# Probabilities of the second attention layer: turned by DMA instead of TensorE, scores first, weighted sums after

## The chip, the cores and the metric

The kernel runs on one core of a Trainium2 chip. The time is the device time of one execution in microseconds (us); three runs of the kernel before are shown by their median. TensorE (PE) multiplies matrices, VectorE (DVE) and ScalarE (ACT) do elementwise work and reductions, GpSimd (POOL) does elementwise work in SBUF, and SyncE (SP) issues the DMAs. Each engine works through its own list of instructions in order, and waits on semaphores for the others.

## The reference, cut to what matters

Eight batch elements of 512 rows with 512 features go through four residual layers. The changed part is the second layer, an attention with one head over a side sequence f:

```python
bias = braak_embed[braak_stages][..., None]
q = query + bias                                  # query = x after layer 0
attn = jnp.einsum('bsd,btd->bst', q, key)         # key = value = f
attn = jax.nn.softmax(attn, axis=-1)
return jnp.einsum('bst,btd->bsd', attn, value)    # added to x
```

Layer 0 is an attention of 16 heads with projections of x and f; layers 2 and 3 are small adapters with a normalization. Their code isn't touched.

## The kernel before

All work of a batch element is cut into 4 tiles of 128 rows. Where products must be exact enough, a float32 operand is kept as a high and a low float16 half, and hi_lo (L451) makes three float16 matmuls per contraction step: four steps, so twelve matmuls for a product of 128 rows by 512 columns.

For each element the engines go through three stages: attention (layer 0), layer1 (the output projection of layer 0 and all of the second layer), and mid (the adapters of this element, woven into the projections of the next). The order inside a stage is a list written by hand that every engine walks, each doing its own part of each step; for layer1 it is ORDER_L1 (L154), and for the last element order_last (L193), where adapter steps follow.

The steps of layer1 for tile t are:

- WOP and WO: output projection of layer 0 on PE; DVE adds it to x1; ACT adds the bias and writes the query tile q1.
- X1T: PE transposes q1 with four float32 transposes into a bank; ACT copies the high half to q1T, DVE subtracts for the low half.
- S1: PE makes the score product of twelve matmuls (a set for each tile) into bank 2 or 3; DVE finds the row maximum; ACT takes the exponential into p1, with the row sum in its accumulator.
- P1T: PE transposes p1 with four float32 transposes into bank 0 or 1 (L1482); ACT copies the high half, scaled, from the bank to p1T (L866); DVE makes the reciprocal of the row sum and subtracts for the low half (L1172).
- PV1: PE makes the weighted sum of twelve matmuls with p1T as the weights (weigh_values, L1233), into bank pair 4 or 6; DVE scales it and adds it to x1 (add_values, L973).

p1 and p1T hold two tiles each and lie in p1_both. A step on PE waits with wait_free for its bank to be read, and with wait_read or wait_full for other steps.

Beside this POOL prepares the next element. split_f (L555) waits until the next x has been turned, and then splits the four side tiles into float16 halves (L493 high, L495 low). SP turns the halves with DMA transposes (turn, L678): turn_tiles (L683) issues four for xT when the output projection has read its old content, waits for the last score product, and issues four for fT, each when POOL has split its tile. The Q product of the next element waits for fT, the K product before it for xT.

Of the kernel before, what the change touches and what calls it, by code (L numbers as in the profile page):

```python
# [18 lines left out]
NT = S // P  # L19
# [56 lines left out]
def order_mid(tail, head):  # L76
# [34 lines left out]
    for i, step in enumerate(slots):  # L111
# [18 lines left out]
        if step == ("VS", 2):  # L130
# [21 lines left out]


ORDER_L1 = ([("WOP", 1), ("WOP", 2), ("WO", 0), ("WO", 1), ("WOP", 3), ("X1T", 0), ("X1T", 1), ("WO", 2),  # L154
             ("WO", 3), ("S1", 0), ("X1T", 2), ("S1", 1), ("X1T", 3), ("P1T", 0), ("S1", 2),
             ("P1T", 1), ("PV1", 0), ("S1", 3), ("P1T", 2), ("PV1", 1), ("P1T", 3), ("PV1", 2), ("PV1", 3)])


def home_banks():

    home = {}
    n = m = 0
    for step in order_mid(False, True):
        if step[0] in ("Q", "K", "KS", "VS", "V"):
            home[step] = n % 2
            n += 1
        elif step[0] == "SMAX":
            home[step] = (4, 6)[m // 2 % 2]
            m += 1
    home.update({("MROW",): 4, ("SROW",): 6, ("PREPB",): 2, ("PREPA",): 3})  # L170
    for g in range(NG):
        home.update({("SELF", g): 3, ("NORMS", g): 2, ("SELFW", g): 3, ("PV", g): g % 2})
        home.update({("ST", g, k, u): (4, 6)[u] for k in range(NT) for u in range(2)})
    for t in range(NT):
        home.update({("WO", t): (4, 6)[t // 2], ("X1T", t): t % 2, ("P1T", t): t % 2, ("S1", t): 2 + t % 2,
                     ("PV1", t): (4, 6)[t % 2], ("NIN", t): (4, 6)[t % 2], ("IN", NT + t): 2 + t % 2})
        home.update({(kind, t): 2 for kind in ("X2T", "HID", "ADP", "X3T", "LOW", "LORA")})
    return home
# [14 lines left out]
def order_last():  # L193

    norm = {t: [("NORM", t, n) for n in range(NORM_PIECES)] for t in (0, 2)}
    cut = ORDER_L1.index(("PV1", 1)) + 1
    return (ORDER_L1[:cut]
            + [("X2T", 0), ("P1T", 3), ("HID", 0), ("X2T", 1), ("PV1", 2), ("ADP", 0), ("HID", 1), ("SQ", 0),
               ("PV1", 3), ("ADP", 1), ("SQ", 1), ("X2T", 2)] + norm[0]
            + [("HID", 2), ("X2T", 3), ("SCALE", 0), ("HID", 3), ("X3T", 0), ("SCALE", 1), ("ADP", 2), ("LOW", 0),  # L200
               ("X3T", 1), ("SQ", 2), ("ADP", 3), ("LOW", 1), ("SQ", 3)] + norm[2]
            + [("LORA", 0), ("LORA", 1), ("SCALE", 2), ("X3T", 2), ("SCALE", 3), ("LOW", 2), ("X3T", 3),
               ("LORA", 2), ("LOW", 3), ("LORA", 3)])
# [37 lines left out]
def build_program(nc, x, f, len_, stage_, lang_, rlang_, Wq, bq, Wk, bk, Wv, bv, Wo, bo, b_prev, b_self,  # L241
                  embed, W1, b1, W2, b2, gamma, beta, lora_A, lora_B, lang_embed, out):
    ctx = ExitStack()
    with ctx:
# [3 lines left out]
        def sem(name):  # L248
            return ctx.enter_context(nc.semaphore(name))
# [55 lines left out]

        aT = xT
        t1, t2 = y[:, 0, :], y[:, 1, :]
        p1 = p1_both[:, 0]
        p1T = p1_both[:, 1].bitcast(F16).rearrange("p a (h k n) -> p a h k n", h=2, k=NT)


        self2 = p1_both[0:H, 0]
# [55 lines left out]
        def read(step, b=0):  # L368
            return free[place(step, b)[0]]
# [57 lines left out]
        sum1 = sem("sum1")  # L427
        rec1 = sem("rec1")
        p1_hi = sem("p1_hi")
        xb_done = sem("xb_done")  # L430
        xg_done = sem("xg_done")
        mean_done = sem("mean_done")
# [150 lines left out]
        def _(eng):  # L583
# [96 lines left out]
                eng.dma_start_transpose(big_t[:, :, :, n * P:(n + 1) * P].rearrange("p h d n -> p (h d) n"),  # L680
                                        split16[:, b % 2, n, :, :].rearrange("p h n -> p (h n)")).then_inc(landed, 16)

            def turn_tiles(i):  # L683
                b = i + 1
                wait_full(eng, ("WO", NT - 1), i)
                for n in range(NT):
                    eng.wait_ge(x_lo, i * NT + n + 1)
                    turn(xT, n, b, xt_in)
                wait_full(eng, ("S1", NT - 1), i)
                for n in range(NT):  # L690
                    eng.wait_ge(f_lo, b * NT + n + 1)
                    turn(fT, n, b, ft_in)

            def prefetch(i):
                for t in range(NT):
# [17 lines left out]
            for i in range(B - 1):  # L713
                params(i)
                prefetch(i)
                language_row(i)
                load_f(i)
                turn_tiles(i)
                mid(True, True, i)
            params(B - 1)  # L720
            language_row(B - 1)
            mid(True, False, B - 1, [step for step in order_last() if step in ADAPTER_STEPS])
            eng.wait_ge(stored, B * NT * 16)


        @block.scalar
        def _(eng):
# [113 lines left out]
            def layer1(i, head, order=ORDER_L1):  # L841
                for step in order:
                    kind = step[0]
                    t = step[-1]
                    if kind == "X1T":
                        wait_full(eng, step, i)
                        eng.activation(q1T[:, t % 2, 0, :, :], bank(step, i)[:, :].rearrange("p (t n) -> p t n", t=ND),
                                       ACT.Copy).then_inc(q1_hi, 1)
                    elif kind == "WO":

                        wait_read(eng, ("PREPA",), i)
                        wait_read(eng, step, i)
                        if t >= 2:

                            wait_full(eng, ("X1T", t - 2), i)
                        eng.activation(q1[:, t % 2, :], x1[:, t, :], ACT.Identity, bias=ecol[:, t:t + 1]
                                       ).then_inc(q1_done, 1)
                    elif kind == "S1":


                        eng.wait_ge(max1, i * NT + t + 1)
                        if t >= 2:
                            wait_full(eng, ("P1T", t - 2), i)
                        eng.activation(p1[:, t % 2, :], bank(step, i)[:, :], ACT.Exp, bias=nmax[:, t % 2:t % 2 + 1],
                                       accum_out=rsum[:, t % 2:t % 2 + 1]).then_inc(read(step, i), 1)
                    elif kind == "P1T":  # L866
                        wait_full(eng, step, i)
                        if t >= 2:
                            wait_full(eng, ("PV1", t - 2), i)
                        eng.activation(p1T[:, t % 2, 0, :, :], bank(step, i)[:, :].rearrange("p (t n) -> p t n", t=NT),  # L870
                                       ACT.Copy, scale=PS).then_inc(p1_hi, 1)


            for n, v in enumerate((bq, bk, bv, b_self, b_prev)):
# [22 lines left out]
        def _(eng):  # L897
# [253 lines left out]
            def layer1(i, head, order=ORDER_L1):  # L1151
                for step in order:
# [12 lines left out]
                    elif kind == "S1":  # L1165
                        wait_full(eng, step, i)
                        if t >= 2:

                            wait_read(eng, ("S1", t - 2), i)
                        eng.tensor_reduce(nmax[:, t % 2:t % 2 + 1], bank(step, i)[:, :], AX_X, ALU.max,  # L1170
                                          negate=True).then_inc(max1, 1)
                    elif kind == "P1T":  # L1172
                        wait_read(eng, ("S1", t), i)
                        eng.tensor_scalar(rrec[:, t:t + 1], rsum[:, t % 2:t % 2 + 1], PS, None, ALU.mult
                                          ).then_inc(sum1, 1)
                        eng.wait_ge(sum1, i * NT + t + 1)
                        eng.reciprocal(rrec[:, t:t + 1], rrec[:, t:t + 1]).then_inc(rec1, 1)
                        eng.wait_ge(p1_hi, i * NT + t + 1)
                        eng.scalar_tensor_tensor(out=p1T[:, t % 2, 1, :, :],
                                                 in0=bank(step, i)[:, :].rearrange("p (t n) -> p t n", t=NT), scalar=PS,  # L1180
                                                 in1=p1T[:, t % 2, 0, :, :], op0=ALU.mult, op1=ALU.subtract
                                                 ).then_inc(read(step, i), 1)
                    elif kind == "PV1":
                        add_values(step, i)

# [17 lines left out]
        def _(eng):  # L1203
# [29 lines left out]
            def weigh_values(step, i):  # L1233

                t = step[1]
                if t == 0:
                    eng.wait_ge(f_lo, i * NT + NT)
                wait_read(eng, ("P1T", t), i)
                wait_free(eng, step, i)
                hi_lo(eng, tile_of(step, i), [(p1T[:, t % 2, 0, k, :], p1T[:, t % 2, 1, k, :]) for k in range(NT)],  # L1240
                      [(split16[:, i % 2, k, 0, :], split16[:, i % 2, k, 1, :]) for k in range(NT)]).then_inc(done(step, i), 1)

            def project(step, part, b, first=False):
# [209 lines left out]
            def layer1(i, head, order=ORDER_L1):  # L1453
                for step in order:
# [20 lines left out]
                    elif kind == "S1":  # L1475
# [3 lines left out]
                        hi_lo(eng, bank(step, i)[:, :],  # L1479
                              [(q1T[:, t % 2, 0, d, :], q1T[:, t % 2, 1, d, :]) for d in range(ND)],  # L1480
                              [(fT[:, 0, d, :], fT[:, 1, d, :]) for d in range(ND)]).then_inc(done(step, i), 1)
                    elif kind == "P1T":  # L1482
                        wait_read(eng, ("S1", t), i)
                        wait_free(eng, step, i)
                        transpose4(step, p1[:, t % 2, :], i)
                    elif kind == "PV1":
                        weigh_values(step, i)

# [44 lines left out]
```

## Time and profile before

| what | value |
|---|---|
| median of 3 runs | 1336.51 us (1336.19 to 1337.59) |
| the profiled execution's own time | 1336.03 us |
| its span in the trace | 1334.2 us |
| PE / DVE / ACT / POOL busy | 95% / 64% / 64% / 37% of the span |
| mean granted PE clock | 0.99 |

Rows give starts in us from the start of the span. The profiled execution is one of many; its time lies 0.48 us below the median. A busy PE counts from the start of a matmul to its modelled end, and matmuls overlap, so the time that a block of matmuls takes is read from the chain of waits, in which each piece lasts until the next one begins.

### The profile page before, as it was taken

To read this page: it belongs to the slowest core of one execution; us is meant where nothing else is said; L and a number is where in the kernel's file an instruction comes from. 1 tells how busy PE (TensorE), PEld (TensorE's weight loads), DVE (VectorE), ACT (ScalarE), POOL (GpSimd) and SP (SyncE) were. 2 spreads that over 40 slices of the span, in tenths; PEclk is the share of its full clock that TensorE was granted. 3 is DMA by queue.
4 is the path that set the end of the run, shared out by engine and by line. 5 is a ranking of instruction groups with operands and counts; after the bars stand their busy time and mean duration, and the time that the engine had idled before them with its cause. 6 is when DMAs were issued, how large, how long until landed. Compare 5 with 4: busy or idle time off the path is not lost.

```text
span 1334.2 us, 19509 instructions
## 1 busy us (share of the span) xinstructions
PE 1271.1 (95%) x6825; PEld 536.7 (40%) x6825; DVE 860.0 (64%) x1544; ACT 847.9 (64%) x1801; POOL 489.0 (37%) x428
## 2 busy tenths in 40 slices
PE   6999999999999999999999999999999999999995
PEld 3332454324543255333553235432454325543252
DVE  4687438864497645975379744887448864497544
ACT  3697428883398735986369753798428883398631
POOL 3434154142531427312462215614154142531114
PEclk8999999999999999999999999999999999999997
DMA  4303222133221332231331423213222034221100
GB/s 160 110 24 106 64 58 67 36 105 88 54 66 49 95 74 54 58 98 56 64 73 40 121 64 50 57 46 113 64 61 66 34 105 95 50 64 60 31 1 32
DMA packets 121295, 90.47 MB, mean 68 GB/s; under 512 B 73514, under 2 KB 94310, under 8 KB 121198
## 3 DMA queue, kind: packets, MB, share of 16 engines
q1 hardware_dynamic: 121136, 89.22, 25.9%
q8 instruction: 55, 0.90, 0.3%
q14 instruction: 42, 0.34, 0.1%
q10 hardware_dynamic: 62, 0.01, 0.0%
HBM read 40.81 MB, written 8.40 MB: 37 GB/s over the span
## 4 chain that ended last, share of the span: by engine, by line
PE 69%; DVE 15%; ACT 12%; issue 2%; DMA 1%; POOL 1%; ACTq 0%; SPq 0%; POOLq 0%; DVEq 0%
PE bank L458 27%; PE banks L458 13%; DVE nmx L1051 9%; ACT big L833 6%; PE bank L1403 6%; PE banks L1387 6%; ACT banks L782 4%; PE banks L1322 4%; PE bank L1230 4%; PE bank L1350 2%; PE bank L1355 2%; PE bank L1377 2%; PE bank L1413 1%; DVE x L1112 1%; DVE big L1108 1%
## 5 line engine op out<-in xcount | busy, mean ns | idle before, releaser
L782 ACT ACTIVATE banks<-banks,nmx 128x512 f32<-128x512 f32 x512 | 341.9, 686 | 28.1 <-DVE nmx L1051 25.8
L1051 DVE TENSOR_REDUCE nmx<-banks 128x1 f32<-128x512 f32 x512 | 329.4, 685 | 35.6 <-PE banks L1322 34.5
L833 ACT ACTIVATE big<-banks 128x1024 f32<-128x1024 f32 x256 | 247.3, 1022 | 44.2 <-PE banks L1387 43.1
L458 PE MATMUL bank<-fT,w_hi 128*128 128x512 f16 x768 | 258.4, 383 | 0.1
L1322 PE MATMUL banks<-KQ 97*128 97x512 f16 x512 | 196.6, 384 | 16.5 <-ACT banks L782 15.6
L1387 PE MATMUL banks<-KQ 98*128 98x512 f16 x512 | 141.0, 382 | 13.4 <-ACT big L833 8.4
L458 PE MATMUL bank<-fT,w_lo 128*128 128x512 f16 x384 | 146.9, 383 | 0.0
L493 POOL TENSOR_TENSOR split<-tiles_in,ones 128x512 f16<-128x512 f32 x60 | 66.0, 1100 | 219.4 <-DMA xT<-split 203.0
L493 POOL TENSOR_TENSOR half<-qk,ones 128x512 f16<-128x512 f32 x64 | 66.5, 1039 | 212.3 <-ACT qk L764 190.9
L1403 PE MATMUL bank<-big,V 128*32 128x512 f32 x1024 | 136.4, 605 | 0.0
L568 POOL TENSOR_TENSOR x<-x,bo_rows 128x512 f32<-128x512 f32 x32 | 39.7, 1273 | 237.7 <-DMA x<-in_x_dram 237.7
L782 ACT ACTIVATION_READ_ACCUMULATOR banks<-banks,nmx 128x1 f32 x512 | 118.5, 231 | 0.0
L458 PEld LDWEIGHTS bank<-fT,w_hi 128*128 128x128 f16 x768 | 75.8, 99 | 81.1 <-issue 15.4
L1322 PEld LDWEIGHTS banks<-KQ 97*128 97x128 f16 x512 | 49.2, 96 | 122.5 <-ACT banks L782 71.9
L1387 PEld LDWEIGHTS banks<-KQ 98*128 98x128 f16 x512 | 34.2, 97 | 137.7 <-ACT big L833 110.5
L458 PE MATMUL bank<-fT,q1T 128*128 128x512 f16 x384 | 88.1, 379 | 0.0
L458 PE MATMUL banks<-split,p_both 128*128 128x512 f16 x384 | 87.0, 379 | 0.0
L458 PE MATMUL bank<-xT,w_hi 128*128 128x512 f16 x256 | 83.6, 383 | 1.8 <-issue 1.8
L458 PE MATMUL bank<-w_hi,xT 128*128 128x512 f16 x256 | 82.6, 379 | 0.0
L540 POOL TENSOR_TENSOR y<-y,gr 128x512 f32<-128x512 f32 x32 | 42.7, 1334 | 97.1 <-DVE y L1014 97.1
L495 POOL TENSOR_TENSOR half<-qk,half 128x512 f16<-128x512 f32 x64 | 75.8, 1184 | 5.0
L458 PE MATMUL banks<-w_hi,xT 128*128 128x512 f16 x256 | 76.3, 380 | 0.0
(151 smaller groups left out, 1849.3 us busy)
## 6 DMA issues: line engine op xcount, KB each, us to landing
KQ<-half SPq DMA_DIRECT2D x384, 64.0 KB, 2.0
tiles_in<-in_x_dram SPq DMA_DIRECT2D x32, 256.0 KB, 7.3
tiles_in<-in_fside_BxSxS_dram SPq DMA_DIRECT2D x32, 256.0 KB, 3.7
x<-in_x_dram SPq DMA_DIRECT2D x8, 1024.0 KB, 5.9
out_dram<-x SPq DMA_DIRECT2D x32, 256.0 KB, 2.1
w<-in_L_cond_W_dram SPq DMA_DIRECT2D x16, 256.0 KB, 4.6
b2r<-in_L_cond_b_dram SPq DMA_DIRECT2D x8, 256.0 KB, 4.5
gr<-in_L_cond_gamma_dram SPq DMA_DIRECT2D x8, 256.0 KB, 5.8
```

What stands on the lines that cost most here:

```text
L458: mm = eng.matmul(out_ap, pairs[n][0], pairs[n][1], start=(first and n == 0), stop=(last and n == len(pairs) - 1))
L493: eng.tensor_tensor(high, src, ones[:, 0:1].to_broadcast([P, S]), ALU.mult).then_inc(high_done, 1)
L495: eng.tensor_tensor(low, src, high, ALU.subtract).then_inc(low_done, 1)
L540: eng.tensor_tensor(y[:, t % 2, :], y[:, t % 2, :], gr[:, :], ALU.mult).then_inc(scaled, 1)
L568: eng.tensor_tensor(x1[:, t, :], x1[:, t, :], bo_rows[:, :], ALU.add).then_inc(x_bo, 1)
L782: eng.activation(bank(step, i)[:, v, :], bank(step, i)[:, v, :], ACT.Exp, bias=nmx[:, t, h:h + 1], accum_out=esum[:, t, h:h + 1]).then_inc ...
L833: eng.activation(big[:, n % 2, 2 * u:2 * u + 2, :], bank(step)[:, :, :], ACT.Exp).then_inc(read(step), 1)
L1051: eng.tensor_reduce(nmx[:, t, h:h + 1], bank(step, i)[:, v, :], AX_X, ALU.max, negate=True).then_inc(max_done, 1)
L1230: mm = eng.transpose(tile_of(step, b)[:, d * P:(d + 1) * P], src[:, d * P:(d + 1) * P], ident[:, :])
L1322: eng.matmul(bank(step, i)[:, v, :], KQ[0:SHIFT_ROW, j, g, 1, t * P:(t + 1) * P], KQ[0:SHIFT_ROW, j, g, 0, :], start=True, stop=True).then ...
L1387: mm = eng.matmul(bank(step)[:, j % 2, :], KQ[0:SHIFT_ROW + 1, j, g, 0, k * P:(k + 1) * P], KQ[0:SHIFT_ROW + 1, j, g, 1, :], start=True, s ...
L1403: mm = eng.matmul(bank(("PV", g))[q, :], V[:, k, g * P + j * DH:g * P + (j + 1) * DH], big[:, n % 2, j, :], start=(k == 0), stop=(k == NT ...
```

## The change

PE doesn't transpose p1 any more. ACT writes the high half and DVE the low half of the scaled probabilities side by side, query-major, into p16 (two tiles), and SP turns each tile with one DMA transpose (128 rows by 1024 float16 values) into p1T, which now has room for four tiles. PE's weighted sum waits for that DMA. The order is all four score products first, with the halving step P1T t right behind the exponential of tile t, and then the four weighted sums. p1 and p16 move to the second half of big, the buffer of layer 0's exponentials, which the adapters use later; p1T takes all of p1_both. In turn_tiles SP issues xT 0 to 3, P1T 0 to 2, fT 0 and 1, P1T 3, fT 2 and 3, in that order, each behind a wait; in the last element only the four of P1T. POOL's code stays the same.

```diff
 ORDER_L1 = ([("WOP", 1), ("WOP", 2), ("WO", 0), ("WO", 1), ("WOP", 3), ("X1T", 0), ("X1T", 1), ("WO", 2),
-             ("WO", 3), ("S1", 0), ("X1T", 2), ("S1", 1), ("X1T", 3), ("P1T", 0), ("S1", 2),
-             ("P1T", 1), ("PV1", 0), ("S1", 3), ("P1T", 2), ("PV1", 1), ("P1T", 3), ("PV1", 2), ("PV1", 3)])
+             ("WO", 3), ("S1", 0), ("X1T", 2), ("P1T", 0), ("S1", 1), ("X1T", 3), ("P1T", 1), ("S1", 2), ("P1T", 2),
+             ("S1", 3), ("P1T", 3), ("PV1", 0), ("PV1", 1), ("PV1", 2), ("PV1", 3)])
...
-            + [("X2T", 0), ("P1T", 3), ("HID", 0), ("X2T", 1), ("PV1", 2), ("ADP", 0), ("HID", 1), ("SQ", 0),
+            + [("X2T", 0), ("HID", 0), ("X2T", 1), ("PV1", 2), ("ADP", 0), ("HID", 1), ("SQ", 0),
...
-        p1 = p1_both[:, 0]
-        p1T = p1_both[:, 1].bitcast(F16).rearrange("p a (h k n) -> p a h k n", h=2, k=NT)
+
+        p1, p16 = big[:, 1, 0:2], big[:, 1, 2:4].bitcast(F16)
+        p1T = p1_both[:].rearrange("p a b n -> p (a b) n").bitcast(F16).rearrange("p t (h k n) -> p t h k n", h=2, k=NT)
...
+        p1_lo = sem("p1_lo")
+        p1t_in = [sem(f"p1t_in{n}") for n in range(NT)]
...
-            def turn_tiles(i):
+            def turn_tiles(i, head):
+
+
                 b = i + 1
-                wait_full(eng, ("WO", NT - 1), i)
-                for n in range(NT):
-                    eng.wait_ge(x_lo, i * NT + n + 1)
-                    turn(xT, n, b, xt_in)
-                wait_full(eng, ("S1", NT - 1), i)
-                for n in range(NT):
-                    eng.wait_ge(f_lo, b * NT + n + 1)
-                    turn(fT, n, b, ft_in)
+                if head:
+                    wait_full(eng, ("WO", NT - 1), i)
+                    for n in range(NT):
+                        eng.wait_ge(x_lo, i * NT + n + 1)
+                        turn(xT, n, b, xt_in)
+                for t in range(NT):
+                    if head and t == NT - 1:
+                        wait_full(eng, ("S1", NT - 1), i)
+                        for n in range(2):
+                            eng.wait_ge(f_lo, b * NT + n + 1)
+                            turn(fT, n, b, ft_in)
+                    eng.wait_ge(p1_lo, i * NT + t + 1)
+                    eng.dma_start_transpose(p1T[:, t, :, :, :].rearrange("p h k n -> p (h k) n"), p16[:, t % 2, :]
+                                            ).then_inc(p1t_in[t], 16)
+                if head:
+                    for n in range(2, NT):
+                        eng.wait_ge(f_lo, b * NT + n + 1)
+                        turn(fT, n, b, ft_in)
...
                         if t >= 2:
-                            wait_full(eng, ("P1T", t - 2), i)
+                            eng.wait_ge(p1_lo, i * NT + t - 1)
                         eng.activation(p1[:, t % 2, :], bank(step, i)[:, :], ACT.Exp, bias=nmax[:, t % 2:t % 2 + 1],
                                        accum_out=rsum[:, t % 2:t % 2 + 1]).then_inc(read(step, i), 1)
                     elif kind == "P1T":
-                        wait_full(eng, step, i)
+                        wait_read(eng, ("S1", t), i)
                         if t >= 2:
-                            wait_full(eng, ("PV1", t - 2), i)
-                        eng.activation(p1T[:, t % 2, 0, :, :], bank(step, i)[:, :].rearrange("p (t n) -> p t n", t=NT),
-                                       ACT.Copy, scale=PS).then_inc(p1_hi, 1)
+                            eng.wait_ge(p1t_in[t - 2], i * 16 + 16)
+                        eng.activation(p16[:, t % 2, 0:S], p1[:, t % 2, :], ACT.Copy, scale=PS).then_inc(p1_hi, 1)
...
-                        eng.scalar_tensor_tensor(out=p1T[:, t % 2, 1, :, :],
-                                                 in0=bank(step, i)[:, :].rearrange("p (t n) -> p t n", t=NT), scalar=PS,
-                                                 in1=p1T[:, t % 2, 0, :, :], op0=ALU.mult, op1=ALU.subtract
-                                                 ).then_inc(read(step, i), 1)
+                        eng.scalar_tensor_tensor(out=p16[:, t % 2, S:2 * S], in0=p1[:, t % 2, :], scalar=PS,
+                                                 in1=p16[:, t % 2, 0:S], op0=ALU.mult, op1=ALU.subtract
+                                                 ).then_inc(p1_lo, 1)
...
-                wait_read(eng, ("P1T", t), i)
+                eng.wait_ge(p1t_in[t], i * 16 + 16)
                 wait_free(eng, step, i)
-                hi_lo(eng, tile_of(step, i), [(p1T[:, t % 2, 0, k, :], p1T[:, t % 2, 1, k, :]) for k in range(NT)],
+                hi_lo(eng, tile_of(step, i), [(p1T[:, t, 0, k, :], p1T[:, t, 1, k, :]) for k in range(NT)],
...
-                    elif kind == "P1T":
-                        wait_read(eng, ("S1", t), i)
-                        wait_free(eng, step, i)
-                        transpose4(step, p1[:, t % 2, :], i)
```

## Rows read from the trace of the kernel before

**Rows 1.** The page: busy time of each engine, share of the span, instructions.

```profile
PE 1271.1 (95%) x6825; PEld 536.7 (40%) x6825; DVE 860.0 (64%) x1544; ACT 847.9 (64%) x1801; POOL 489.0 (37%) x428
```

**Rows 2.** Chain of waits, element 1: start, us until the next piece, what.

```profile
313.40 2.59 PE bank L458 x12
315.99 0.44 PE bank L1230 x4
...
331.56 5.18 PE banks L458 x24
```

**Rows 3.** Busy time by engine in the stage; then granted clock, DMA share, GB/s.

```profile
313.40:336.74 23.34, 23.34 (x121) 12.19 (x120) 11.26 (x24) 7.48 (x16) 9.88 (x9) 1.00 0.48 91
```

**Rows 4.** Timeline of element 1's stage: start us, duration us, engine, line, operation.

```profile
312.33 1.29 DVE L1163 TENSOR_TENSOR q1T<-bank,q1T 128x512 f16<-128x512 f32 x2 [2.24 <-ACT q1T L847]
...
313.08 2.42 PEld L458 LDWEIGHTS bank<-fT,q1T 128*128 128x128 f16 x12 [0.17 <-DVE q1T L1163]
...
316.03 0.69 DVE L1170 TENSOR_REDUCE nmax<-bank 128x1 f32<-128x512 f32 x1 [1.21 <-PE bank L458]
...
316.75 0.69 ACT L864 ACTIVATE p_both<-bank,nmax 128x512 f32<-128x512 f32 x1 [1.11 <-DVE nmax L1170]
317.34 0.19 ACT L864 ACTIVATION_READ_ACCUMULATOR p_both<-bank,nmax 128x1 f32 x1
317.43 0.59 ACT L847 ACTIVATE q1T<-bank 128x512 f16<-128x512 f32 x1
...
321.68 0.14 DVE L1174 TENSOR_SCALAR rrec<-rsum 128x1 f32<-128x1 f32 x1
...
321.94 0.67 DVE L1179 SCALAR_TENSOR_TENSOR p_both<-bank,p_both 128x512 f16<-128x512 f32 x1
```

**Rows 5.** DVE beside POOL: one line's min/median/max ns, then timelines of attention.

```profile
L1136 DVE SCALAR_TENSOR_TENSOR xT<-y,cols,xT x32: 750/751/1532, 123.6 to 1265.3; 128x512 f16<-128x512 f32 x32
...
283.72 1.53 DVE L1136 SCALAR_TENSOR_TENSOR xT<-y,cols,xT 128x512 f16<-128x512 f32 x1
...
283.48 1.22 POOL L495 TENSOR_TENSOR split<-tiles_in,split 128x512 f16<-128x512 f32 x1
284.66 1.48 POOL L493 TENSOR_TENSOR split<-tiles_in,ones 128x512 f16<-128x512 f32 x1
...
762.39 1.36 DVE L1134 TENSOR_SCALAR xT<-y,cols 128x512 f16<-128x512 f32 x1
...
762.43 1.04 POOL L493 TENSOR_TENSOR split<-tiles_in,ones 128x512 f16<-128x512 f32 x1 [2.65 <-DMA tiles_in<-in_x_dram]
```

**Rows 6.** Timeline of POOL in the stage, the first two of eight splits.

```profile
320.75 1.04 POOL L493 TENSOR_TENSOR split<-tiles_in,ones 128x512 f16<-128x512 f32 x1 [28.89 <-DMA xT<-split]
...
321.86 1.16 POOL L495 TENSOR_TENSOR split<-tiles_in,split 128x512 f16<-128x512 f32 x1
```

**Rows 7.** Groups by line: busy us, mean ns; idle before. ACT from SBUF.

```profile
L856 ACT ACTIVATE q<-x,ecol 128x512 f32<-128x512 f32 x32 | 21.7, 721 | 70.6 <-DVE x L1158 58.5 <-issue 12.1
```

**Rows 8.** SP's timeline, and the time to landing of the fT transposes.

```profile
313.43 5.45 SPq L680 DMA_TRANSPOSE xT<-split  x4
...
DMA to landing us min/median/max: 3.1/3.3/5.2
```

**Rows 9.** Chain of waits, element 7.

```profile
1290.42 0.45 PE bank L1230 x4
...
1291.64 1.13 PE bank L1350 x8
```

**Rows 10.** PE's idle time and granted clock: stretches as in rows 3, one timeline row.

```profile
1302.00:1305.00 3.00, 1.60 (x12) 1.36 (x12) 1.86 (x11) 1.68 (x5) 1.07 (x1) 1.00 0.00 0
...
51.73 0.39 PE L1322 MATMUL banks<-KQ 97*128 97x512 f16 x1 [2.51 <-ACT banks L782]
...
52.00:53.00 1.00, 1.00 (x5) 0.60 0.36 88
...
55.00:56.00 1.00, 1.00 (x4) 0.69 0.00 0
```

More of the change, by code:

```diff
@@ L174, in home_banks @@
     for t in range(NT):
-        home.update({("WO", t): (4, 6)[t // 2], ("X1T", t): t % 2, ("P1T", t): t % 2, ("S1", t): 2 + t % 2,
+        home.update({("WO", t): (4, 6)[t // 2], ("X1T", t): t % 2, ("S1", t): 2 + t % 2,
                      ("PV1", t): (4, 6)[t % 2], ("NIN", t): (4, 6)[t % 2], ("IN", NT + t): 2 + t % 2})
@@ L717, in _ @@
                 load_f(i)
-                turn_tiles(i)
+                turn_tiles(i, True)
                 mid(True, True, i)
@@ L721, in _ @@
             language_row(B - 1)
+            turn_tiles(B - 1, False)
             mid(True, False, B - 1, [step for step in order_last() if step in ADAPTER_STEPS])
```

## The prediction

> **What bounds the kernel now.** The engine line of the page comes first: TensorE (PE) is busy for 95% of the span, and nothing else comes near it [rows 1]. That is an average, so I went to the stage that is changed. The chain of waits through the second layer of the second batch element (element 1) is matmul after matmul without a gap: the first score product starts at 313.40, and the last two weighted sums start at 331.56 and end 5.18 later, at 336.74. The stage lasts 23.34 us; a block of twelve matmuls costs 2.59 and a set of four transposes 0.44 [rows 2]. The stretch view says the same from the other side: PE 23.34 of 23.34 us busy, its clock at 1.00, the 16 DMA engines at 0.48 for eight DMA transposes [rows 3]. So PE's work bounds this stage; what is taken from PE is won only as far as nothing else becomes later than PE. I work in the times of element 1; its pattern repeats in elements 0 to 6, and element 7 is taken by itself.
>
> **What goes.** Four sets of P1T transposes leave each element: 4 x 0.44 = 1.74 us (unrounded 0.435). Work left for PE in the stage: 23.34 - 1.74 = 21.60 us. If nothing waited, eight elements would save 13.9 us. The new work is off PE; ACT and DVE had the two halving operations before, on a PSUM source. Their new place in the order, the new source, and the DMA decide.
>
> **First wait: the fourth score product.** The first score product ends at 315.99. DVE's maximum starts at 316.03 and takes 0.69; ACT's exponential starts at 316.75, and its accumulator read ends at 317.53, which is when its semaphore fires: 0.78 [rows 4]. A semaphore step costs 0.03 to 0.05. The copy of query tile 2 starts at 317.43 and takes 0.59; then DVE subtracts, 318.05 to 318.74 (two such in 1.29 [rows 4]: each 0.69, the second starting 0.60 after the first, an overlap of 0.08). New is that P1T 0 now stands here in DVE's order, before the second maximum: two tiny operations (0.26 from the first to the subtraction behind them [rows 4]) and the subtraction itself, 318.92 to 319.67 at 0.75, the median of the one operation in the trace with the same operands (SBUF f32 and f16 into f16) [rows 5]. The maximum of tile 1 thus starts at 319.58 and not at 319.05, ACT's exponential at 320.30, the copy of query tile 3 ends at 321.57, its subtraction at 322.29. PE has finished the third product at 322.05 (X1T 2, X1T 3 and three products after 313.40). From a weight load released by DVE to the block's start in the chain is 313.40 - 313.08 = 0.32 [rows 2, 4]; with 0.05 for the semaphore the fourth product starts at 322.66: **0.61 idle**. It ends at 325.25.
>
> **The DVE-POOL port.** From 320.75, when the next element's xT transposes have landed, POOL splits the side tiles: eight instructions of 1.04 and 1.16 us, nearly without pause [rows 6]. Before, the low half read PSUM and one SBUF tensor, and took 0.67 beside POOL [rows 4]. Now it reads two SBUF tensors. What that costs next to POOL is seen in the attention stage: the DVE instruction at 283.72, normally 0.75, took 1.53, and ended 0.55 after POOL's instruction of 283.48 to 284.70; POOL's next took 1.48 instead of 1.04 [rows 5]. So the two take turns, whole instructions at a time. The bounds for one subtraction are 0.75 and 1.53.
>
> P1T 1's subtraction asks at 322.47, inside POOL's 321.86 to 323.02, and so ends at 323.02 + 0.55 = 323.57. Anything from 321.86 to 323.02 gives that end, which makes it robust. POOL's following two then run to 324.46 and 325.70, and the next one begins at 325.66. Meanwhile: maximum of tile 2 from 323.49, exponential from 324.21, its semaphore at 324.99, the f16 copy from 325.03. That copy now reads SBUF. The bounds are 0.59 (the PSUM copy) and 0.72 (the Identity from SBUF [rows 7]); I take 0.62, nearer the plain copy. P1T 2's subtraction then asks at 325.68, next to POOL's 325.66. This is the closest call of the whole sum. I take POOL first: any longer copy makes that certain, and at 762.39 a DVE instruction begun 0.04 before a POOL one still took 1.36, while POOL took its plain 1.04 [rows 5]. P1T 2 then ends at 326.70 + 0.55 = 327.25.
>
> **Second wait: SP's queue.** A DMA transpose occupies SP for 1.36 us (four in 5.45) and lands 3.3 us after its issue (3.1 to 5.2) [rows 8]. P1T 0 is issued at 319.7, behind the four xT transposes, and lands at 323.0; P1T 1 goes out at 323.6 and lands at 326.9. Both are hidden under the score products: the weighted sums start at 325.25 and 327.84 with no wait, and ACT's new waits for the landings of tiles 0 and 1 cost nothing. P1T 2 goes out at 327.30. Behind it in SP's order stand two fT transposes, whose data are ready (POOL's second split ends at 325.70), and only then P1T 3: issue at 327.30 + 3 x 1.36 = 331.38, landing at 334.68, weighted sum 3 from 334.68 + 0.37 = 335.05. DVE isn't the later one here: P1T 3's subtraction meets the port like the one before and ends at 331.05.
>
> Weighted sum 2 has a wait of its own. Its bank is freed by the first DVE add, which now stands behind P1T 3's subtraction: 330.97 to 331.72. PE would have been ready at 330.43 and starts at 332.07: **1.64 idle**, until 334.66; then **0.39** until 335.05. The end is 335.05 + 2.59 = 337.64.
>
> **Sum.** 21.60 of work and 0.61 + 1.64 + 0.39 = 2.64 of waits make 24.24, against 23.34: +0.90 per element, +6.3 for seven. The fT transposes 2 and 3 land at 337.4; what needs them stands behind the twelve matmuls of the first K product (to 340.2), so a lateness of up to 2.8 us stays covered there. Moving the buffers into big costs nothing: its old readers are done before the stage, its next writers come after it. In element 7 there is no split and no fT transpose, so only the first wait is left. Ahead of X2T 0 (now at 1290.42) three sets of transposes go, 1.31, and 0.61 of idle comes; the fourth set goes for nothing, since it sits in the gap in which the hidden product at 1291.64 waits for ACT's copy of X2T 0 [rows 9]. That gives 0.61 - 1.31 = -0.70. In total +5.6. The profiled execution took 1336.03 us, 0.48 below the median of 1336.51; on the median the sum is **1342.1**.
>
> One rule of the Trainium skill weighs on this (VectorE: DVE Perf Modes, The three transpose paths): it gives 390 ns for a 128x128 bf16 transpose on TensorE and 1309 ns on the DMA crossbar, and prefers TensorE where PSUM will do, which speaks against this change. The trace has 0.44 us for four f32 blocks on PE and 3.3 for a DMA transfer of eight f16 blocks; were the landing 1.31, weighted sum 3 would wait for weighted sum 2 alone (end 337.25), and the sum would be 1339.4.
>
> **Rivals.**
> *DVE takes the port first at 325.68.* P1T 2 ends at 326.43, P1T 3 lands at 333.86, the stage ends at 336.82: +0.08, 7 x 0.08 - 0.70 = -0.1, 1336.4. For it: the two starts are 0.02 apart. Chance 0.27.
> *PE stays the bound (the other side).* If transposes and port let weighted sums 2 and 3 start when PE reaches them, only 0.61 is lost: 7 x (0.61 - 1.74) - 0.70 = -8.6, 1327.9. It decides if P1T 3 lands before 332.6, 2.1 earlier than worked out; the shortest landing of 3.1 gives 0.2 of that. Chance 0.10.
> *No port conflict at all*: P1T 2 at 326.08, stage end 336.47, -0.27 each, 1333.9. The 1.53 speaks against it. Chance 0.07, at the edge of what can be told from no change.
> *Both subtractions at 1.53, or landings near 4.* P1T 2 at 327.64, +1.29 each, 1344.8 and somewhat more. Chance 0.12.
> *The clock drops.* A wait of 2.51 us before 51.73 was followed by a granted clock of 0.50, its lower level, while 1302 to 1305, with PE idle nearly half the time, stayed at 1.00; the low level lasted from about 52.2 to 55.6, some three us of work [rows 10]. The waits here are 1.64 and 0.39 with work between. Three us of work at half clock lose 1.5; in seven elements that gives 1352.6. Chance 0.06.
>
> **The numbers.** Forecast 0.38. A measurement of this kernel tells about 0.2% (2.7 us) from no change. Faster: 0.10 and half of 0.07, 0.13. Same: 0.27 and the other half, 0.31. Slower: 0.38 + 0.12 + 0.06 = 0.56. The forecast alone spans 1340.7 (landings at 3.1, 7 x 0.70 - 0.70) to 1344.8. The range must take in the tie and the case without the port, and the upper bound with some late landings: 1333 to 1346, leaving out the fast rival and the clock.
>
> **What would show it.** In the profile after: a gap of some 0.6 before the fourth score product, released by DVE's q1T; P1T 2's low half on DVE over 1 us and ended by a POOL instruction; PE's wait before weighted sum 2 on DVE's add and before weighted sum 3 on the DMA; stages of 24.2 us in elements 0 to 6, and X2T 0 of element 7 about 0.7 nearer to its first score product. I am wrong if the low halves all take 0.75, if P1T 3 is issued before the fT transposes finish issuing, if it lands in under 2 us, or if the clock column falls below 1.00 within the stage.

## The result and the profile after

The changed kernel takes 1342.64 us (median of 5 runs, 1340.92 to 1344.37) against 1336.26 of the kernel before in its 5 runs: a ratio of 1.0052, interval 1.0040 to 1.0063. It is slower by 6.4 us, clear of noise. The forecast was 1342.1. Line numbers shift: L462 is hi_lo, L684 and L703 are SP's transposes, L1195 is DVE's low half, L996 its add, L497 and L499 are POOL's splits.

The page of the kernel after answers to [rows 1]:

```profile
PE 1260.7 (94%) x6697; PEld 519.9 (39%) x6697; DVE 874.0 (65%) x1544; ACT 849.7 (63%) x1801; POOL 495.3 (37%) x428
```

PE has 128 transposes and some 10 us of busy time less, and the kernel is longer all the same: what PE gave back became idle time, and more. DVE is 14 us busier with the same number of instructions. The stretch of element 1's stage (from the first score product to the first K matmul), columns as in [rows 3], and the last pieces of its chain of waits:

```profile
312.44:336.45 24.01, 22.08 (x105) 10.11 (x104) 13.36 (x24) 7.72 (x16) 10.69 (x9) 1.00 0.69 132
```

```profile
328.35 1.16 POOL split L499
329.51 0.77 SPq L684
330.28 0.04 issue
330.33 3.32 DMA p_both<-big
333.64 0.05 issue
333.69 2.76 PE banks L462 x12
336.45 0.43 PE bank L462 x2
```

The stage took 23.34 before, unbroken PE work. Now it takes 24.01, the clock is still at 1.00, and the chain no longer runs through PE: it comes from POOL's splits over SP's queue and the landing of P1T 3. Rows from the timeline of the same stage, for DVE, POOL, PE and PE's weight loads (PEld):

```profile
317.94 0.67 DVE L1195 SCALAR_TENSOR_TENSOR big<-big 128x512 f16<-128x512 f32 x1
...
318.52 0.68 DVE L1186 TENSOR_REDUCE nmax<-bank 128x1 f32<-128x512 f32 x1
...
320.88 1.16 POOL L499 TENSOR_TENSOR split<-tiles_in,split 128x512 f16<-128x512 f32 x1
...
321.28 2.27 PEld L462 LDWEIGHTS bank<-fT,q1T 128*128 128x128 f16 x12 [0.71 <-DVE q1T L1179]
321.29 2.76 PE L462 MATMUL bank<-fT,q1T 128*128 128x512 f16 x12 [0.22 <-DVE q1T L1179]
...
321.41 1.18 DVE L1195 SCALAR_TENSOR_TENSOR big<-big 128x512 f16<-128x512 f32 x1
...
324.68 1.04 POOL L497 TENSOR_TENSOR split<-tiles_in,ones 128x512 f16<-128x512 f32 x1
324.69 1.57 DVE L1195 SCALAR_TENSOR_TENSOR big<-big 128x512 f16<-128x512 f32 x1 [0.31 <-ACT big L887]
...
328.35 1.15 POOL L499 TENSOR_TENSOR split<-tiles_in,split 128x512 f16<-128x512 f32 x1
328.37 1.68 DVE L1195 SCALAR_TENSOR_TENSOR big<-big 128x512 f16<-128x512 f32 x1 [0.31 <-ACT big L887]
329.97 1.40 DVE L996 SCALAR_TENSOR_TENSOR x<-banks,rrec,x 128x512 f32<-128x512 f32 x2
...
330.86 5.60 PE L462 MATMUL banks<-split,p_both 128*128 128x512 f16 x24 [1.62 <-DVE x L996]
```

Three things are to be seen, in order of time: PE waits for the fourth score product because DVE's maximum at 318.52 stands behind P1T 0's low half; the low halves of tiles 1 to 3 take 1.18, 1.57 and 1.68 us beside POOL, the first takes 0.67 without it; and PE's long wait, for weighted sum 2 at 330.86, is for the add that DVE does only after the last low half. (A number in brackets is counted from the modelled end of the matmul before, and so is 0.16 to 0.17 smaller than the time by which a block starts late.) SP in that stage:

```profile
312.45 5.44 SPq L684 DMA_TRANSPOSE xT<-split  x4
318.64 8.89 SPq L703 DMA_TRANSPOSE p_both<-big  x3
327.62 2.66 SPq L684 DMA_TRANSPOSE fT<-split  x2
330.33 1.34 SPq L703 DMA_TRANSPOSE p_both<-big  x1
331.71 2.71 SPq L684 DMA_TRANSPOSE fT<-split  x2
```

P1T 3 could go out only when its low half was done (330.05) and SP had issued the two fT transposes ahead of it (until 330.28): the two lie 0.2 us apart, and the chain follows the later one.

The stage lengths of elements 0 to 6, from PE's timeline, are 24.22, 24.03, 25.46, 24.39, 24.27, 24.07 and 23.98 us: 7.0 us more than seven times 23.34. Element 7 gains 0.5. Together that is +6.5, and the medians differ by 6.4. The two profiled executions differ by only 4.9 (spans of 1339.1 and 1334.2): in the one after, the first score product of element 0 starts at 151.59 and not at 153.45. That lead, ahead of everything that the change touches, runs from 150.9 to 157.8 us over the nine profiled executions, so lengths of stages can be compared between them, and single spans only roughly.

### The profile page after: what moved, and what is told of

Read it like the earlier page. It is cut to its first block, busy times and chain, and to the rows that moved or that the text cites. A ratio compares the mean times of both kernels' runs of the same rounds, so it can differ in the third digit from the quotient of the medians.

```text
span 1339.1 us, 19253 instructions
## 1 busy us (share of the span) xinstructions
PE 1260.7 (94%) x6697; PEld 519.9 (39%) x6697; DVE 874.0 (65%) x1544; ACT 849.7 (63%) x1801; POOL 495.3 (37%) x428
## 4 chain that ended last, share of the span: by engine, by line
PE 57%; DVE 16%; ACT 13%; DMA 4%; POOL 4%; SPq 2%; issue 2%; ACTq 0%; POOLq 0%; DVEq 0%
PE bank L462 21%; DVE nmx L1067 9%; PE banks L462 8%; ACT big L850 6%; PE bank L1418 6%; PE banks L1402 6%; ACT banks L799 5%; PE banks L1337 4%; DMA p_both<-big 2%; PE bank L1245 2%; SPq L684 2%; PE bank L1365 2%; PE bank L1370 2%; POOL split L499 2%; POOL split L497 2%
## 5 line engine op out<-in xcount | busy, mean ns | idle before, releaser
L462 PE MATMUL bank<-fT,w_hi 128*128 128x512 f16 x768 | 256.8, 380 | 0.3 <-DVE prod L1059 0.3
L497 POOL TENSOR_TENSOR split<-tiles_in,ones 128x512 f16<-128x512 f32 x60 | 68.9, 1149 | 220.7 <-DMA xT<-split 204.4
L462 PE MATMUL bank<-fT,w_lo 128*128 128x512 f16 x384 | 145.9, 380 | 0.0
L497 POOL TENSOR_TENSOR half<-qk,ones 128x512 f16<-128x512 f32 x64 | 66.8, 1044 | 202.5 <-ACT qk L781 178.8
L462 PEld LDWEIGHTS bank<-fT,w_hi 128*128 128x128 f16 x768 | 75.4, 98 | 79.9 <-issue 13.5
L462 PE MATMUL banks<-split,p_both 128*128 128x512 f16 x384 | 87.2, 379 | 14.2 <-DVE x L996 11.4
L462 PE MATMUL bank<-fT,q1T 128*128 128x512 f16 x384 | 88.2, 379 | 1.8 <-DVE q1T L1179 1.8
L462 PE MATMUL bank<-xT,w_hi 128*128 128x512 f16 x256 | 84.0, 384 | 1.3 <-issue 1.3
L462 PE MATMUL bank<-w_hi,xT 128*128 128x512 f16 x256 | 82.6, 379 | 0.0
L499 POOL TENSOR_TENSOR half<-qk,half 128x512 f16<-128x512 f32 x64 | 75.7, 1184 | 5.0
L462 PE MATMUL banks<-w_hi,xT 128*128 128x512 f16 x256 | 76.3, 380 | 0.0
```

The lines of the kernel that those rows point to most:

```text
L462: mm = eng.matmul(out_ap, pairs[n][0], pairs[n][1], start=(first and n == 0), stop=(last and n == len(pairs) - 1))
L497: eng.tensor_tensor(high, src, ones[:, 0:1].to_broadcast([P, S]), ALU.mult).then_inc(high_done, 1)
L499: eng.tensor_tensor(low, src, high, ALU.subtract).then_inc(low_done, 1)
```

## The experiments

Theory A: the stage is PE work as long as nothing is late; the low half, moved to two SBUF operands, takes turns with POOL's splits, and this lateness reaches PE through DVE's add and through P1T 3. Theory B: the DMA, by its latency or by its place in SP's queue, is the cause. Theory C: the new order is what costs.

| kernel | median us | ratio to before (interval) | stage, element 1 |
|---|---|---|---|
| before | 1335.3 to 1336.3 | 1 | 23.34 |
| changed | 1342.64 | 1.0052 (1.0040 to 1.0063) | 24.03 |
| P1T 3 ahead of fT | 1340.29 | 1.0034 (1.0022 to 1.0046) | 23.78 |
| exponentials in PSUM | 1332.57 | 0.9978 (0.9968 to 0.9988) | 22.63 |
| both | 1325.79 | 0.9926 (0.9914 to 0.9939) | 22.07 |
| POOL hardly splits | 1333.00 | 0.9976 (0.9965 to 0.9987) | 22.77 |
| changed, old order | 1413.32 | 1.0586 (1.0567 to 1.0605) | waits of 4.7, 3.5 and 1.5 |
| both, and DVE's order | 1322.60 | 0.9903 (0.9887 to 0.9920) | 21.62 |
| before, scores first | 1337.32 | 1.0010 (0.9997 to 1.0024) | 23.33 |

The first score product's start to the first K matmul's start in PE's timeline is the stage here. The kernel before was run again beside the experiments, and each ratio is to the runs beside it.

**P1T 3 ahead of the fT transposes** (on the changed kernel):

```diff
                 for t in range(NT):
-                    if head and t == NT - 1:
-                        wait_full(eng, ("S1", NT - 1), i)
-                        for n in range(2):
-                            eng.wait_ge(f_lo, b * NT + n + 1)
-                            turn(fT, n, b, ft_in)
                     eng.wait_ge(p1_lo, i * NT + t + 1)
...
                 if head:
-                    for n in range(2, NT):
+                    wait_full(eng, ("S1", NT - 1), i)
+                    for n in range(NT):
```

> The changed kernel with one edit on SP's queue: P1T 3 is issued before the fT transposes, which all four follow it. Theory A (what I read in the trace after: P1T 3's low half is done on DVE only at 330.05, after a port wait, and SP is free for it at 330.29): SP's order costs only about 0.2 us per element in elements 0 to 6, so 1.4 us less than the changed kernel, about 1341 against 1336.3 of before, still slower than before. Theory B (the two fT transposes in SP's queue are the cause, as the prediction put it for weighted sum 3): P1T 3 lands 2.7 us earlier, weighted sum 3 follows weighted sum 2 without a wait and some 0.3 to 1.0 us per element come back, down to 1336 to 1340.

Measured 1340.29, some 2.4 us less than the changed kernel by the two ratios, whose intervals overlap. The time alone doesn't decide, since it lies between the two expectations. The stage lost 0.25 us in element 1, as theory A said, and 0.31 on average over elements 0 to 6 (0.02 to 0.72). The timeline shows why it isn't more: the low half of tile 3 ends only at 329.31, and weighted sum 2 still waits for the add behind it.

```profile
327.63 1.68 DVE L1191 SCALAR_TENSOR_TENSOR big<-big 128x512 f16<-128x512 f32 x1 [0.31 <-ACT big L883]
329.24 1.40 DVE L992 SCALAR_TENSOR_TENSOR x<-banks,rrec,x 128x512 f32<-128x512 f32 x2
...
330.12 5.34 PE L462 MATMUL banks<-split,p_both 128*128 128x512 f16 x24 [1.62 <-DVE x L992]
```

So SP's order by itself cost little here, since the data of P1T 3 were hardly ready earlier.

**Exponentials in PSUM** (on the changed kernel). The exponential is written in place into the score product's bank, so the low half has one SBUF operand. ACT's copy for the high half reads the bank too. Score products 2 and 3 take banks 0 and 1, which P1T had before, and the bank is freed by the low half:

```diff
-        home.update({("WO", t): (4, 6)[t // 2], ("X1T", t): t % 2, ("S1", t): 2 + t % 2,
+        home.update({("WO", t): (4, 6)[t // 2], ("X1T", t): t % 2, ("S1", t): (2, 3, 0, 1)[t],
...
-                        eng.activation(p1[:, t % 2, :], bank(step, i)[:, :], ACT.Exp, bias=nmax[:, t % 2:t % 2 + 1],
+                        eng.activation(bank(step, i)[:, :], bank(step, i)[:, :], ACT.Exp, bias=nmax[:, t % 2:t % 2 + 1],
...
-                        eng.scalar_tensor_tensor(out=p16[:, t % 2, S:2 * S], in0=p1[:, t % 2, :], scalar=PS,
+                        eng.scalar_tensor_tensor(out=p16[:, t % 2, S:2 * S], in0=bank(("S1", t), i)[:, :], scalar=PS,
```

> The changed kernel, but the exponentials stay in the score product's PSUM bank (written in place; score products 2 and 3 move to the two banks that P1T left), so that the low half reads PSUM and one SBUF tensor and not two SBUF tensors. Theory A (the DVE-POOL port is the main cost): low halves 1, 2 and 3 fall from 1.2, 1.6 and 1.7 us to 0.7, the wait of weighted sum 2 for DVE's add goes, weighted sum 3 still waits about 0.4 us for P1T 3, whose issue stands behind two fT transposes. Stage 22.6 us against 23.34 of before: 7 x -0.8 - 0.5, about 1330. Theory B (the DMA's latency by itself is what costs): no more than 1 us of change, about 1342.

Measured 1332.57, ratio 0.9978: already faster than before. The low half's line (minimum, median, maximum in ns over 32), first in the changed kernel, then here:

```profile
L1195 DVE SCALAR_TENSOR_TENSOR big<-big x32: 671/1256/1686, 157.3 to 1293.5; 128x512 f16<-128x512 f32 x32
```

```profile
L1195 DVE SCALAR_TENSOR_TENSOR big<-bank,big x32: 671/682/693, 159.3 to 1283.8; 128x512 f16<-128x512 f32 x32
```

PE in element 1 of this kernel runs three weighted sums without a wait, and only the last waits, for the DMA:

```profile
324.41 7.93 PE L462 MATMUL banks<-split,p_both 128*128 128x512 f16 x36
332.74 2.76 PE L462 MATMUL banks<-split,p_both 128*128 128x512 f16 x12 [0.40 <-DMA p_both<-big]
```

The stage of element 1 is 22.63, as expected (22.6). The total came out 2 to 3 us above the expected 1330: elements 2 and 4 took 23.84 and 23.43. There the chain of waits shows P1T 3 landing 4.55 and 4.14 us after its issue, and PE's wait before the last weighted sum is 1.60 and 1.19 us (in brackets) instead of 0.40.

**Both edits.**

> Both edits: exponentials in PSUM, and P1T 3 issued before the fT transposes. Theory A: no wait is left on PE but the one before the fourth score product (0.4 us); stage 22.0 us, 7 x -1.35 - 0.5 = -10, about 1326, faster than both kernels. If the DMA's latency is the cost whatever the port does: 1340 or more.

Measured 1325.79: 9.9 us less than before by the ratio, and all seven stages are 22.07 us long. In elements 0 to 6 the weighted sums run on without a wait. PE in element 1, and SP's issue of P1T 3:

```profile
318.55 2.75 PE L462 MATMUL bank<-fT,q1T 128*128 128x512 f16 x12 [0.32 <-DVE q1T L1175]
321.13 10.52 PE L462 MATMUL banks<-split,p_both 128*128 128x512 f16 x48
...
324.80 1.23 SPq L698 DMA_TRANSPOSE p_both<-big  x1
```

P1T 3 landed 3.2 us after its issue in all seven elements of this execution, so a late landing was not put to the test here. An estimate: weighted sum 3 starts at 328.90 (321.13 and three blocks of 2.59), 4.10 after the issue of P1T 3 at 324.80, so a landing after 4.7 would cost some 0.6. In element 7, P1T 1 did land late (4.8 us), and PE waited 0.41 for it.

SP's order, worth 0.25 us in element 1 beside the port conflict, is worth 0.56 there (22.63 to 22.07) without it: which wait ends last decides what an edit is worth. In elements 2 and 4 the stage lost more (23.84 and 23.43 to 22.07), but there the late landings of the one execution are missing in the other, and that is not shown to be the edit's doing: with P1T 3 ahead alone, it landed 5.0 us after its issue in element 2.

**POOL hardly splits** (on the changed kernel). POOL splits 8 of the 512 columns of each side tile of the next element; the rest of the split is left out. The low half still reads two SBUF tensors:

```diff
-                    split(split16[:, b % 2, n, 0, :], split16[:, b % 2, n, 1, :], tiles_in[:, n, :],
-                          f_hi, b * NT + n + 1, f_lo)
+                    at = slice(0, 8)
+                    eng.tensor_tensor(split16[:, b % 2, n, 0, at], tiles_in[:, n, at], ones[:, 0:1].to_broadcast([P, 8]),
...
```

> The changed kernel; POOL splits only 8 of the 512 columns of each side tile of the next element, so elements 1 to 7 get wrong side data and POOL leaves the shared port free during the second layer. Nothing else is changed: the low half still reads two SBUF tensors. Theory A: the low halves take 0.7 us, PE's wait for DVE's add goes, as in the kernel with the exponentials in PSUM: about 1330. If the second SBUF operand itself is slow, or the wait is not POOL's: about 1342.

Measured 1333.00, the same as with the exponentials in PSUM. The low half takes 0.69 with both operands in SBUF, so it isn't the second SBUF operand that is slow, but POOL's work at the same time (here 0.20 us an instruction, and all over by 321 us in element 1):

```profile
L1199 DVE SCALAR_TENSOR_TENSOR big<-big x32: 672/692/709, 158.2 to 1284.9; 128x512 f16<-128x512 f32 x32
```

**The changed kernel in the old order** (ORDER_L1 and order_last of the kernel before; the DMA transposes stay):

```diff
-             ("WO", 3), ("S1", 0), ("X1T", 2), ("P1T", 0), ("S1", 1), ("X1T", 3), ("P1T", 1), ("S1", 2), ("P1T", 2),
-             ("S1", 3), ("P1T", 3), ("PV1", 0), ("PV1", 1), ("PV1", 2), ("PV1", 3)])
+             ("WO", 3), ("S1", 0), ("X1T", 2), ("S1", 1), ("X1T", 3), ("P1T", 0), ("S1", 2),
+             ("P1T", 1), ("PV1", 0), ("S1", 3), ("P1T", 2), ("PV1", 1), ("P1T", 3), ("PV1", 2), ("PV1", 3)])
```

> The changed kernel with the order of the kernel before: the DMA transposes stay, but the weighted sums 0 and 1 stand between the score products again. Theory A (the landing of a DMA transpose, 3.3 us behind a later low half, is only hidden because all score products come first): weighted sum 0 waits for P1T 0 nearly 5 us, weighted sum 2 or 3 for P1T 2 and 3 some 3 us more, and TensorE's clock may fall behind such waits. About 7 us per element more than before: 1385 to 1410. Theory C (the order is what costs, the DMA is free): below 1336.

Measured 1413.32, a little above the expected range. In element 1 weighted sum 0 waits 4.7 us, until 3.1 after the issue of P1T 0 (SP's row), and weighted sum 2 3.5 us. While PE is idle before weighted sum 0, from 330.42 on, the granted clock (the fourth of the columns in the second fence: stretch and length, busy time of PE, clock) falls from 1.00 to its lower level, 0.50, and in the wait before weighted sum 2 it stays at 1.00. SP's and PE's timeline, then PE's stretches:

```profile
331.94 15.21 SPq L703 DMA_TRANSPOSE p_both<-big  x3
...
335.08 5.28 PE L462 MATMUL banks<-split,p_both 128*128 128x512 f16 x12 [4.66 <-issue]
...
349.16 2.77 PE L462 MATMUL banks<-split,p_both 128*128 128x512 f16 x12 [3.46 <-DMA p_both<-big]
```

```profile
332.00:334.00 2.00, 0.00 (x0) 0.93 0.46 90
334.00:336.00 2.00, 0.92 (x3) 0.50 0.31 58
336.00:338.00 2.00, 2.00 (x6) 0.50 1.29 113
338.00:340.00 2.00, 2.00 (x6) 0.50 0.05 9
340.00:342.00 2.00, 2.00 (x9) 0.86 0.00 0
...
346.00:348.00 2.00, 0.00 (x0) 1.00 0.48 93
348.00:350.00 2.00, 0.84 (x4) 1.00 0.95 180
```

The twelve matmuls of weighted sum 0 took 5.28 us instead of 2.75. So scores first isn't what costs: it is what hides the landing, and without it the kernel with the DMA route is 78 us slower than the kernel before, waits and clock together. The port has little part in that, since the low half's median here is 0.69.

**Both edits and DVE's order.** On DVE alone the maximum of score product 1 goes ahead of P1T 0's low half:

```diff
+            def for_dve(order):
+                order = list(order)
+                n = order.index(("P1T", 0))
+                order[n:n + 2] = [("S1", 1), ("P1T", 0)]
+                return order
```

> The kernel with both edits (exponentials in PSUM, P1T 3 ahead of the fT transposes), and on DVE alone the maximum of score product 1 goes ahead of P1T 0's low half; ACT and PE keep their order. If the 0.4 us that PE still waits for before the fourth score product comes from DVE's order, it goes in all eight elements: 3 us less than the kernel with both edits, about 1323. If it doesn't come from there: 1326.

Measured 1322.60, ratio 0.9903, the fastest of all. Every stage is 21.62 or 21.63 us long, which is PE's own work of 21.60: no wait is left. So the place of P1T 0 ahead of the second maximum in DVE's list, a part of the new order, did cost 0.45 us a stage. The stretch of element 1 and its chain:

```profile
310.90:332.50 21.60, 21.60 (x106) 10.25 (x104) 11.19 (x24) 7.59 (x16) 9.88 (x9) 1.00 0.71 135
```

```profile
313.49 0.44 PE bank L1247 x4
313.93 2.59 PE bank L462 x12
316.52 0.44 PE bank L1247 x4
316.96 5.21 PE bank L462 x24
322.17 10.36 PE banks L462 x48
```

**Scores first alone** (on the kernel before, TensorE still transposes, p1T has room for four tiles and p1 lies in big). It isn't the list of the change step by step: P1T 0 stands behind the second score product, and P1T 3 behind weighted sum 0:

```diff
+             ("WO", 3), ("S1", 0), ("X1T", 2), ("S1", 1), ("X1T", 3), ("P1T", 0), ("S1", 2), ("P1T", 1), ("S1", 3),
+             ("P1T", 2), ("PV1", 0), ("P1T", 3), ("PV1", 1), ("PV1", 2), ("PV1", 3)])
```

> The kernel before with the order part of the change alone: all four score products first, p1T with room for four tiles, but TensorE still makes the transposes and the low half reads PSUM. Theory A (PE's work bounds the stage as long as nothing is late): stage 23.3 us as before, about 1336. Theory C (scores first makes DVE's adds or the low halves late by itself): stage over 24 us, 1341 or more.

Measured 1337.32, ratio 1.0010 with 1 inside the interval; the stages of elements 0 to 6 are 23.33 to 23.35. Its ten runs spread from 1335.1 to 1343.3; in the profiled one, 1341.82, it is the lead to the first score product that is long (157.84). Putting the scores first does nothing to a stage that is all PE work. Theory C falls so far, and holds for one detail of the new list, the place of P1T 0 on DVE.

## Why the prediction was right

The sum and its signs held, and its terms were sized nearly right; that the total came within 0.5 us is in part luck (see what the sum left out). In element 1, idle time from PE's timeline (what a block starts later than the block before it would have let it):

| step | predicted us | measured us |
|---|---|---|
| before the fourth score product | 0.61 | 0.39 |
| before weighted sum 2, for DVE's add | 1.64 | 1.79 |
| before weighted sum 3, for P1T 3 | 0.39 | 0.25 |
| stage against before | +0.90 | +0.69 |
| element 7 | -0.70 | -0.48 |

**First wait.** Right in place and releaser (DVE's q1T), and 0.22 too large. P1T 0's low half, taken as 0.75 from the nearest row, took 0.67 where POOL was quiet and let the next maximum begin 0.58 after its start: that is 0.08. The rest is the step from a weight load released by DVE to its block, 0.32 in the sum: in PE's timeline the first matmul starts 0.01 after the load (321.28 and 321.29), while at the first score product it starts 0.16 after it (312.10 and 312.26). What PE didn't lose here it lost at the second wait, whose end, set by DVE's add, came within 0.1 of the working; hence 1.79 there and not 1.64.

**The port.** This was the closest call, and it came out as written: in element 1 POOL's split starts at 324.68 and DVE's low half at 324.69, and DVE waits through the whole of POOL's instruction. The same happened at tiles 2 and 3 in all seven elements, at 1.57 to 1.69 us, with POOL 0.01 to 0.02 ahead each time. The working had this tie at 0.02, and it goes back to tile 1, whose low half ends 0.54 to 0.55 after the POOL instruction that it met, whenever it asked; which side a tie of 0.02 falls on was luck as much as working. The kernel in the old order has the other outcome, in element 6:

```profile
1185.20 0.67 DVE L1195 SCALAR_TENSOR_TENSOR big<-big 128x512 f16<-128x512 f32 x1
1185.21 1.56 POOL L497 TENSOR_TENSOR split<-tiles_in,ones 128x512 f16<-128x512 f32 x1 [31.08 <-DMA xT<-split]
```

There DVE starts 0.01 ahead and takes its plain 0.67, and POOL's instruction takes 1.56 instead of 1.04. Two experiments that take the conflict away in different ways, by the operand and by POOL's work, give the same time, 1332.6 and 1333.0, so the port is shown as the cause of the largest wait. The Trainium skill (SBUF — State Buffer, SBUF: two separate sides) says that a DVE instruction with two SBUF inputs and a GpSimd instruction that reads SBUF exclude each other for a whole instruction, and that the one that starts first has it; the low halves here agree, down to 0.01 us of start. The row at 762.39 [rows 5], on which the prediction leaned, doesn't bear on them: that DVE instruction is a TENSOR_SCALAR with one 128x512 source, and why it lost although 0.04 ahead is open. The rival in which DVE goes first, and the one without a conflict, thereby fell.

**SP's queue.** The issue of P1T 3 behind two fT transposes was as worked out (2.66 us for the two, then a landing of 3.32). The prediction gave it no more than what is left beside the other wait, and that held: taken away alone it gives 0.25 us in element 1. The experiments show the port as the larger part: taking it away alone brings 1.4 us there. The two are not one: without the port the wait for the add is gone, and the wait for P1T 3 behind the two fT transposes is 0.56.

**What the sum left out.** Element 2's stage is 25.46, 1.3 us above the others: P1T 3 landed 4.7 us after its issue instead of 3.3:

```profile
491.62 4.72 DMA p_both<-big
```

The bounds of the landing had this, and so did one of the rivals (landings near 4), which came true in one element of seven; the central sum did not. Element 7 lost 0.42 in the same way: weighted sum 1 waited for a P1T 1 that landed 4.7 us after its issue, and without that the saving there would have been some 0.9 and not 0.48. So seven stages came to +7.0 where the sum had +6.3, of which 1.3 is one late landing: without it they would have come to some +5.7. That two kinds of error, terms somewhat too large and a landing left out, nearly cancel is luck; the kinds of wait and their order are not.

**The landing.** The Trainium skill's 1.31 us on the DMA crossbar (VectorE: DVE Perf Modes, The three transpose paths) is for one 128x128 block. No landing so short was seen: the transfers of P1T, eight blocks each, land after 3.0 to 4.7 us, with a median of 3.2. The preference of the Trainium skill for TensorE (same page, Rules for kernel authors), which spoke against the change, held for the kernel as it was changed and not for the mechanism: with the waits removed the same DMA transposes make the kernel 1.0% faster.

**The clock.** The rival didn't come: with single waits of up to 2.0 us every stage of the changed kernel kept a granted clock of 1.00. In the kernel in the old order it did come, within the wait of 4.66 us in element 1, and not in the one of 3.46 us there.

Of the 13.9 us that eight elements could save if nothing waited, the last version gets 13.0 by its ratio (0.0097 x 1336).

## What to carry to other kernels

Work that is taken off the bounding engine is only won if what replaces it arrives in time; list for each new step what stands before it on its engine and in its DMA queue, and follow that to the engine that bounds. Before moving a source from PSUM to SBUF look at what GpSimd does at that moment: here a VectorE instruction with two SBUF operands took up to 1.69 us beside it instead of 0.67, and leaving one operand in PSUM took that away. A change that comes out slower for a nameable wait is not yet refuted: three small repairs, each for one wait that the trace named, turned 0.5% slower into 1.0% faster.

## What the runs showed that was not expected

The port conflict locks itself in. From the low half of tile 2 to that of tile 3 (maximum, exponential, copy, subtraction between them) it is 3.68 us in element 1, and three of POOL's instructions, one of them itself held up by DVE, take 3.67. So after the first meeting the two ask for the port within 0.02 us of each other again, and DVE loses both times. That the two chains are equally long is a coincidence of this kernel's instructions.

Late landings come back at the same places. P1T 3 of element 2 takes 4.6 to 5.0 us instead of 3.2 and makes that stage the longest in the changed kernel (25.46), with P1T 3 ahead (25.44), with the exponentials in PSUM (23.84) and with POOL hardly splitting (24.03); with both edits and in the last version it lands after 3.2. P1T 1 of element 7 takes 4.0 to 4.8 in the first five of these kernels and 3.1 in the last. What delays these transfers is open; no run was made for it.
